# Four decoder layers with mixtures of experts: routing by 16-bit counts, one scan and one-hots in fours; first gathers inside the route; a flat norm; the mask joined with the row extreme

## The reference

```python
x = x + _L0_xattn_ref(_layernorm(x), ctx, ctx, ...)
x = x + _L0_ffn_ref(_layernorm(x), ...)     # 8 experts, 2 per row, and a shared expert
x = x + _L1_xattn_ref(_layernorm(x), ctx, ...)
x = x + _L1_ffn_ref(_layernorm(x), ...)     # 8 experts, 1 per row, bias on the router
x = x + _L2_xattn_ref(_layernorm(x), ctx, ctx, mask, ...)
x = x + _L2_ffn_ref(_layernorm(x), ...)     # two groups of 32 experts, 2 per row in each
x = x + _L3_xattn_ref(_layernorm(x), ctx, ctx, ...)
x = x + _L3_ffn_ref(_layernorm(x), ...)     # 32 experts, 1 per row, capacity 80 rows
```

```python
attn0 = jnp.where(mask, 0.0, attn).reshape(1, B * H, T, T)
attn = lax.conv_general_dilated(attn0, kernels, ..., feature_group_count=B * H, ...)
attn = jnp.where(mask, -jnp.inf, attn)
p = jax.nn.softmax(attn, axis=-1)
```

```python
expert_weights, expert_indices = lax.top_k(scores, top_k)
order = jnp.argsort(expert_indices.reshape(-1))
tok = jnp.repeat(jnp.arange(T), top_k)[order]
xs = x2[tok]
ys = lax.ragged_dot(jax.nn.silu(lax.ragged_dot(xs, wg, group_sizes))
                    * lax.ragged_dot(xs, wu, group_sizes), wd, group_sizes)
return jnp.zeros_like(x2).at[tok].add(ys * flat_w[order][:, None])
```

## Time and profile before

| | us |
|---|---|
| median of three runs | 2562.77 |
| profiled execution | 2561.07 |
| its span, first to last instruction | 2559.4 |
| TensorE matmul busy | 2060.4 (81%) |
| TensorE weight load busy | 1682.8 (66%) |
| VectorE busy | 1321.1 (52%) |
| ScalarE busy | 833.2 (33%) |
| GpSimd busy | 741.0 (29%) |

### The profile page before, as it was taken

The page is one execution under the profiler, slowest core; times in us unless marked ns, Lnnn a source line. Parts: engine busy times, 40 slices in busy tenths (PEclk is TensorE's granted clock), DMA queues, the critical chain, the costliest instruction groups (busy, mean ns, idle before and its releaser), DMA issues. The chain is left out here.

```text
span 2559.4 us, 42188 instructions
## 1 busy us (share of the span) xinstructions
PE 2060.4 (81%) x13649; PEld 1682.8 (66%) x13743; DVE 1321.1 (52%) x3816; ACT 833.2 (33%) x2012; POOL 741.0 (29%) x933
## 2 busy tenths in 40 slices
PE   6869979892799999999689847995794963787694
PEld 5657746661799988998579825664683852454594
DVE  3542225524687778887400065764546545675523
ACT  4613213412133333333323323443241432345321
POOL 1022100005344444443111032210455744231133
PEclk9869989985899999999789968996795986899797
DMA  2052130002211111100189634436377563442384
GB/s 79 9 206 63 52 113 13 1 1 86 79 34 37 42 43 38 40 22 1 40 324 347 229 109 125 129 87 231 90 154 281 159 123 100 118 125 58 136 298 167
DMA packets 142727, 280.72 MB, mean 110 GB/s; under 512 B 20160, under 2 KB 99008, under 8 KB 138432
## 3 DMA queue, kind: packets, MB, share of 16 engines
q1 hardware_dynamic: 125824, 232.49, 26.7%
q0 software_dynamic: 16704, 45.64, 7.6%
HBM read 218.94 MB, written 56.62 MB: 108 GB/s over the span
## 5 line engine op out<-in xcount | busy, mean ns | idle before, releaser
L1983 PE MATMUL heads_ps_c<-heads_band,heads_sT 128*128 128x129 f32 x3072 | 367.5, 276 | 15.1 <-DVE heads_band L2201 12.1
L1983 PEld LDWEIGHTS heads_ps_c<-heads_band,heads_sT 128*128 128x128 f32 x3072 | 362.2, 192 | 22.9 <-issue 18.9
L2139 POOL TENSOR_SCALAR heads_band<-heads_shifts,heads_taps 128x130 f32<-128x130 f32 x384 | 253.5, 675 | 268.8 <-PE heads_ps_c L1983 265.2
L1042 POOL DMA_INDIRECT experts_xg<-xn_rows,token_of x165 | 161.1, 976 | 298.9 <-PE experts_ps_x L1055 143.0
L2201 DVE SCALAR_TENSOR_TENSOR heads_band<-heads_shifts,heads_taps,heads_band 128x130 f32<-128x130 f32 x768 | 226.5, 350 | 31.7 <-POOL heads_band L2139 27.0
L2076 ACT ACTIVATE heads_probs<-heads_ps_c,heads_negmax 128x256 f32<-128x256 f32 x256 | 107.3, 470 | 371.2 <-DVE heads_negmax L2210 371.2
L1726 DVE TENSOR_REDUCE heads_negmax<-heads_ps_m 128x2 f32<-128x512 f32 x256 | 169.6, 688 | 79.7 <-PE heads_ps_m L1582 77.3
L1683 ACT ACTIVATE heads_probsT<-heads_ps_e 128x512 f32<-128x512 f32 x256 | 147.0, 596 | 193.3 <-PE heads_ps_e L1606 193.0
L1196 POOL DMA_INDIRECT combine_yg<-y_rows,slot_of x80 | 75.7, 946 | 332.7 <-SPq L66 309.3
L1066 PE MATMUL experts_ps_g<-weights_w,experts_xT 128*128 x504 | 133.6, 389 | 0.3 <-issue 0.2
L1089 PE MATMUL experts_ps_y<-weights_w,experts_hT 128*128 (+1 forms) x486 | 132.7, 382 | 1.1 <-DVE experts_y L1151 1.1
(11 more groups left out here) (389 smaller groups left out, 4442.9 us busy)
## 6 DMA issues: line engine op xcount, KB each, us to landing
experts_w<-in_experts_dram SPq DMA_DIRECT2D x23, 2180.0 KB, 10.0
weights_w<-in_experts_dram SPq DMA_DIRECT2D x16, 1536.0 KB
weights_w<-in_experts_dram SPq DMA_DIRECT2D x32, 768.0 KB, 7.4
y_rows<-experts_y SPq DMA_DIRECT2D x188, 128.0 KB, 2.2
piece_rows<-heads_pieces SPq DMA_DIRECT2D x96, 192.0 KB, 2.3
heads_stackQ<-piece_rows SPq DMA_DIRECT2D x48, 192.0 KB
heads_stackK<-piece_rows SPq DMA_DIRECT2D x48, 192.0 KB
weights_w<-in_experts_dram SPq DMA_DIRECT2D x8, 1088.0 KB
```

Source lines behind the costliest of these rows:

```text
L1042: pool.indirect_dma_start(xg[:, j % ahead, :], None, xn_dram, bass.IndirectOffsetOnAxis(ap=tb.token_of[:, j:j + 1], axis=0))\
L1983: last = pe.matmul(out[:, qc * SEQ + k0:qc * SEQ + k1], sT[:, h % 2, kc, qc * P + dq:qc * P + dq + P], band[:, h % 2, dq, w0:w0 + k1 - k0] ...
L2139: last = pool.tensor_scalar(band[:, h % 2, dq, :], shifts[:, 0, :], taps[:, r % 2, h, dq * TAPS:dq * TAPS + 1], None, ALU.mult)
```

## The change

Routes: hot becomes bf16 and lies by expert (tiles innermost); the triangle becomes `since`, 0 or -1, also bf16, so that running total plus product is the position. The count product comes first, and the zeroing of the token sum ahead of the wait. The 16 adds become one `tensor_tensor_scan` over E x 16 numbers, with a factor `restart` that is 0 at each expert's first tile. The one-hots are made four columns at a time by three instructions, double-buffered, the loop unrolled. slot_of, the capacity's mask and the tile experts come behind. POOL gathers the first three tiles of rows inside the route, as soon as token_of is there; the buffer `xg` and its semaphores belong to `FirstRows`, outside both stages.

Layer 2: the norm uses the pieces of the other norms, in groups of four tiles (`RowNorm`, L220). The weights have 40 slots; the first 8 experts of group 1 are loaded at the start of experts2_0, the other 24 in route2_1. 20 of the 32 late gathers stand in route2_1, and 12 in experts2_1 between POOL's row gathers; group 1 writes its outputs to a DRAM buffer of its own.

Convolution heads: the mask product goes. VectorE's reduction becomes two `tensor_tensor_reduce` per head, which add the mask (f32 in SBUF), write `mixes` to SBUF and take the minimum; the sign of q is turned so that the minimum is what was the negated maximum, and the exp has scale -1. TensorE's convolution waits for the row step of two heads before (`maxed`) and no longer for its exp; the row step waits for the exp of two heads before.

In the route, first TensorE's block, then VectorE's:

```diff
-            flat = hot[:, :, :].rearrange("p t e -> p (t e)")
-            pe.matmul(ps_pos.rearrange("p t e -> p (t e)"), tb.before[:, :], flat)
-            pe.matmul(ps_all.rearrange("p t e -> p (t e)"), ones[:, :], flat).then_inc(counted, 1)
-            out = ps_tok[:, 0:NT]
-            pe.sem_inc(perm_used, 4)
-            pe.matmul(out, ones[:, :], tb.zeros[:, 0:NT], start=True, stop=False, skip_group_check=True)
-            with pe.Fori(0, NK // 4) as i:
-                for p in range(4):
-                    pe.wait_ge(perm_ready, 4 * i + p + 1)
-                    pe.matmul(out, lane_hot[:, p, :], tile_hot[:, p, :], start=False, stop=False,
-                              skip_group_check=True).then_inc(perm_used, 1)
+            flat = hot[:, :, :].rearrange("p e t -> p (e t)")
+            pe.matmul(ps_all, tb.ones16[:, :], flat).then_inc(counted, 1)
+            pe.matmul(ps_pos, tb.since[:, :], flat).then_inc(placed, 1)
+            for c in range(NK // CH):
+                pe.wait_ge(chunk_ready, c + 1)
+                for n in range(CH):
+                    last = pe.matmul(out, lane_hot[:, c % 2, n, :], tile_hot[:, c % 2, n, :], start=False, stop=False,
+                                     skip_group_check=True)
+                last.then_inc(chunk_used, 1)
...
-                v.tensor_tensor(hot[:, :, :], hot_k[:, 0, :, :], hot_k[:, 1, :, :], ALU.add)\
+                v.tensor_tensor(by_tile(hot[:, :, :]), hot_k[:, 0, :, :], hot_k[:, 1, :, :], ALU.add)\
                     .then_inc(hot_ready, 1)
...
             v.wait_ge(counted, 1)
-            for t in range(TILES):
-                steps.done(v.tensor_tensor(earlier[:, t + 1, :], earlier[:, t, :], ps_all[:, t, :], ALU.add))
-            steps.done(v.tensor_tensor(pos[:, :, :], ps_pos[:, :, :], earlier[:, 0:TILES, :], ALU.add))
+            steps.done(v.tensor_tensor_scan(upto[:, :, :].rearrange("p e t -> p (e t)"),
+                                            tb.restart[:, 0:E * TILES], ps_all, 0.0, ALU.mult, ALU.add))
+            v.wait_ge(placed, 1)
+            steps.done(v.tensor_tensor(pos[:, :, :].rearrange("p e t -> p (e t)"), ps_pos,
+                                       upto[:, :, :].rearrange("p e t -> p (e t)"), ALU.add))
```

The one-hots, the tail of the route and the first rows:

```diff
+            for c in range(NK // CH):
+                if c >= 2:
+                    v.wait_ge(chunk_used, c - 1)
+                n = slice(CH * c, CH * (c + 1))
+                th, lh = tile_hot[:, c % 2, :, :], lane_hot[:, c % 2, :, :]
+                v.tensor_tensor(th, tb.row_iota[:, 0:NT].unsqueeze(1).to_broadcast([P, CH, NT]),
+                                hi[:, n].unsqueeze(2).to_broadcast([P, CH, NT]), ALU.is_equal).then_inc(own, 1)
+                steps.n += 1
+                v.tensor_tensor(lh, tb.row_iota[:, :].unsqueeze(1).to_broadcast([P, CH, P]),
+                                lo[:, n].unsqueeze(2).to_broadcast([P, CH, P]), ALU.is_equal)
+                v.wait_ge(own, steps.n)
+                v.tensor_tensor(th, th, tb.token_id[K][:, n].unsqueeze(2).to_broadcast([P, CH, NT]), ALU.mult)\
+                    .then_inc(chunk_ready, 1)
...
-            with v.Fori(0, NK // 4) as i:
-                for p in range(4):
-                    n = 4 * i + p
-                    v.wait_ge(perm_used, n + 1)
-                    v.tensor_scalar(tile_hot[:, p, :], tb.row_iota[:, 0:NT], hi[:, bass.ds(n, 1)],
-                                    tb.token_id[K][:, bass.ds(n, 1)], ALU.is_equal, ALU.mult)
-                    v.tensor_scalar(lane_hot[:, p, :], tb.row_iota[:, :], lo[:, bass.ds(n, 1)], None,
-                                    ALU.is_equal).then_inc(perm_ready, 1)
+            v.wait_ge(summed, 1)
+            v.tensor_copy(tb.token_of[:, 0:NT], ps_tok[:, 0:NT]).then_inc(token_ready, 1)
+            if capacity is None:
+                steps.done(v.tensor_tensor(ended[:, :, :], tiles_end[:, :].unsqueeze(1).to_broadcast([P, NT, E]),
+                                           tb.row_iota[:, 0:NT].unsqueeze(2).to_broadcast([P, NT, E]),
+                                           ALU.is_le))
+                steps.done(v.reduce_sum(tile_expert[:, :], ended[:, :, :], X))
+                steps.done(v.tensor_scalar(tile_expert[:, :], tile_expert[:, :], float(E - 1), float(P),
+                                           ALU.min, ALU.mult))
+                v.tensor_scalar(tb.weights_of[:, 0:NT], tile_expert[:, :], tb.column[:, 0:1], None, ALU.add)
...
+        @block.gpsimd
+        def _(pool):
+            if late is not None:
+                late.gather(pool, 0, late.EARLY, gathered)
+            if xn is not None:
+                pool.wait_ge(xn_stored, 16)
+            pool.wait_ge(token_ready, 1)
+            for j in range(first.COUNT):
+                first.gather(pool, tb, xn_dram, j)
+            if late is not None:
+                pool.wait_ge(gathered, 16 * late.EARLY)
```

The convolution heads and the late rows:

```diff
-                pe.wait_ge(exped, n + 1)
-                pe.matmul(out, ident16[:, :], mask_add[:, :], start=True, stop=False, skip_group_check=True)
+                if not (isinstance(i, int) and n < 2):
+                    pe.wait_ge(maxed, n - 1)
                 pe.wait_ge(masked, n + 3)
...
                 act.wait_ge(turned, n + 1)
                 for qc in range(QC):
-                    last = act.activation(probs[:, h % 2, qc, :], ps_c[:, h % 2, qc * SEQ:(qc + 1) * SEQ], ACT.Exp,
-                                          bias=negmax[:, h % 2, qc:qc + 1])
+                    last = act.activation(probs[:, h % 2, qc, :], mixes[:, h % 2, qc, :], ACT.Exp,
+                                          bias=least[:, h % 2, qc:qc + 1], scale=-1.0)
...
                 v.wait_ge(convolved, n + 3)
-                v.tensor_reduce(negmax[:, h % 2, :], ps_c[:, h % 2, :].rearrange("p (k n) -> p k n", k=QC), X,
-                                ALU.max, negate=True).then_inc(maxed, 1)
+                v.wait_ge(exped, n + 1)
+                v.sem_inc(rows_passed, 1)
+                for qc in range(QC):
+                    last = v.tensor_tensor_reduce(out=mixes[:, h % 2, qc, :], in0=ps_c[:, h % 2, qc * SEQ:(qc + 1) * SEQ],
+                                                  in1=mask_add[:, qc, :], scale=1.0, scalar=-NEG_BIG,
+                                                  op0=ALU.add, op1=ALU.min, accum_out=least[:, h % 2, qc:qc + 1])
+                last.then_inc(maxed, 1)
...
+            for j in range(first.COUNT, NT):
+                first.gather(pool, tb, xn_dram, j)
+                if late is not None and j % 3 == 0 and late.EARLY <= j // 3 + late.EARLY - 2 < 2 * TILES:
+                    late.gather(pool, j // 3 + late.EARLY - 2, j // 3 + late.EARLY - 1, late_in)
...
+                                   ident, ones, prefetch=lambda sp: resident.load(sp, i["experts2_1"], 0, 8, 0))
...
+            first.again(NT)
+            route_stage(core, "route2_1", logits[:, :, 32:64], 32, 2, NT, tb, ones, None, xn_dram, first, factor=0.5,
+                        prefetch=lambda sp: resident.load(sp, i["experts2_1"], 8, 32, 8), late=late)
+            resident_experts_stage(core, "experts2_1", NT, 32, [P], resident, 0, tb, first, xn_dram, y_second,
```

427 lines of the change are left out of this document (190 added, 237 removed).

## The result

The changed kernel takes 2539.24 us (median of four runs, 2534.96 to 2542.26), the kernel before 2562.63 us beside it: a ratio of 0.9899, 95% interval 0.9888 to 0.9911. That is 23 us faster, 0.9 to 1.1%. The forecast was 2505 us with a range of 2490 to 2532, so the direction was right, and the gain was 40% of what was forecast. The profiled execution is the slowest of the four runs, and has a span of 2540.5 us against 2559.4.

A forecast was written before the change was run, and what follows sets the result against it. No engine bounds the whole: TensorE paces heads1, VectorE's chain most of a route, TensorE its one-hot loop. Terms -19 - 6.6 - 1 - 8.6 - 15.8 - 5.7 - 0.5 + 0.5 = -56.7 gave 2505 us, range 2490 to 2532.

The forecast's parts named there:

- The mask in heads1: Convolution heads: one bf16 product per head goes, saving TensorE 1.28 us per round over 16 rounds; 19 us taken.
- +0.28: heads1: VectorE's extra us per head for two add-and-min with accumulator reads; bounds +0.1 (free reads) to +0.75.
- Both rivals that put VectorE at the bound: heads1: +0.75 us per head, 2516 to 2533 (chance 0.20); add-and-min at scan rate, +1.11, 2555 to 2590 (0.07).
- the one on the clock: Routes' one-hot loop: TensorE granted 2.4 GHz, total 2494 us; faster than 2495, by this or other waits going, 0.11.
- The first of those rivals: heads1: mask hidden or VectorE the bound at 4.19 us per head, saving down to about a third; chance 0.20.
- The routes up to the one-hots: route2_0 before the loop: 16-bit counts -2.47 us, scan -2.26, tile experts moved behind tokens -4.98; sum -9.9.
- I take nothing: Routes: strided write of hot and reads of pos counted at 0; bounded by doubling three 0.69 us instructions, +2 us.
- the later of the two plus some 1.2 us of barrier: Route's end: stage ends after the later of three gathers' issue and VectorE's tile experts, plus 1.2 us; route2_0 -8.6 altogether.
- The second tile: Experts behind a route: the second tile's 1.39 us wait for its rows goes; -1.2 in layer 2, -1.0 in route0, route3.
- Layer 2's experts: 12 late gathers between experts2_1's row gathers and 3 MB of prefetch in experts2_0 cost +0.5 us, 0 to +2.
- -14.6 to TensorE: route2_1: TensorE starts at 1969.4 instead of 1984.05, with 20 late gathers ahead and 24 experts loaded; -15.8 with second tile.
- Norm: Layer 2's norm: groups of four let TensorE start some 3 us sooner but add waits; -0.5, between +2 and -2.

## Why the prediction was wrong

- **The mask in heads1** (-19): right in mechanism and size. The add-and-min is the 425 ns row's, 420 ns. Its read is one instruction more and costs nothing: two of them come to 0.35 us of pitch each, 0.1 us more per head than the 0.60 of the one reduction (VectorE's busy time per head is 396.12 / 112.5 = 3.52 us, it was 3.44): the lower bound, and not +0.28. TensorE's saving, forecast at 1.28 us a round, was 1.23 in the mean. Both rivals that put VectorE at the bound fell, and so did the one on the clock: the loop took 13.73 us at 0.50 again. The first of those rivals was also priced wrong: 4.19 us per head is 33.5 a round against 34.50, which leaves three quarters of the 1.28 us and not a third, unless waits come on top. (Its 482 and 196 ns are 484 and 195 in the earlier trace rows.)
- **The routes up to the one-hots**: the counts, the scan and the tile experts behind the tokens were right. The step that failed is "I take nothing" for the strides. In route2_0 they cost 1.61 us on hot and 0.67 on picked, 2.3 us in all: above the bound of +2. Over the five routes the same two instructions are 6.6 us longer than in the trace of before, by their durations. The bound itself was wrong, as it took a doubling for the worst, and the write more than tripled. The trace bears out the rule of the Trainium skill that the prediction weighed ("Advanced Engine Details and Errata", "Memory Cachelines"), at 2.30 against 0.69 us.
- **The end of the route**: the step "the later of the two plus some 1.2 us of barrier" failed. It took a gather as done when GpSimd had issued it, but the stage's end waits until its rows have landed. The next stage starts 2.9 to 3.7 us after the last gather, and the first gather lasted 1.3 to 1.8 us longer. TensorE starts 8.46 us behind the tokens in route2_0 where 6.2 was forecast, and 9.15 in route2_1. In routes 0 and 3 it is 7.6 and 7.5 us where before had 4.5 and 4.7, which takes back over half of what VectorE's shorter chain gave. In **route1** the weights are issued 8.0 us behind the tokens, where it was 1.7: so the gain of 4.2 us turned into +1.5.
- **The second tile** (-1.2 in each): right where it was named; the wait of 1.39 us is gone. What came late next was not named: the fourth tile, by 2.37 us.
- **Layer 2's experts** (+0.5, "0 to +2"): the largest failure. It was worked out from POOL's pace and from bytes. The prefetch cost 3.9 us by standing ahead of small transfers on the same queues, and the late gathers 9.0 us, 7.8 of which went when the padding's rows were spread. Both are over the bound. Together they are 12.9 us, 12.4 more than the +0.5, of the 37.8 missing.
- **route2_1** (-14.6 to TensorE): -10.3. The tokens came 8.1 us sooner instead of 9.4, and the end of the route took the rest. That the early rows and the smaller load would free the queues in time was right: TensorE was released by the barrier, not by a transfer.
- **Norm** (-0.5): -1.6, within its bounds.
- **The range**: each term was given its own bounds, but the rivals were nearly all about heads1. No rival said that the five routes' gain is spent at their ends. One cause there, five times, is not five small independent errors. No row that the prediction used has three gathers outstanding at a barrier, and that called for a bound as wide as a transfer's own latency: in the earlier trace rows the first rows let TensorE start 2.85 us after their gather began (1816.25 to 1819.10).

## What to carry to other kernels

Work that is moved ahead of a barrier is not free because its engine is idle: a gather that is still in flight holds the barrier (here about 3 us), and in these runs it paid only where a larger transfer would otherwise stand ahead of it, and then by under 1 us. Large loads belong where nobody waits for a small transfer; count the stores behind them as well as the gathers. Look at what padding does to a memory: spread addresses that no result depends on.

## What was not expected of the hardware

- A stage's end behind outstanding indirect gathers of GpSimd: 2.9 to 3.7 us after the last one's issue ends, with three of them, 3.45 with one in route3, 0.7 us without any. GpSimd's DRAIN ends 0.08 or 0.09 us behind the landing of the last rows with one gather in the stage, 0.16 or 0.17 with three, 0.98 or 0.99 with 23 (route2_1) and 2.49 with 60 (the changed kernel's experts2_0).
- A gather's issue on GpSimd during a comparison of 128x2016 f32 with two inputs in SBUF: 2.24 and 2.71 us, against 0.95 to 0.99 without it or beside a reduction of 2.25 us with one input.
- A bf16 write of 512 elements with a stride of 32 bytes: 2.30 us against 0.69. An f32 read with a stride of 64 bytes: 0.98 against 0.64. A bf16 moving operand of TensorE, 512 columns with a stride of 64 bytes: 1.02 against 0.61.
- Gathers of 128 times the same row: DMA share 0.82 to 0.92 at 101 to 141 GB/s, against 0.46 at 135 GB/s for 128 different rows.
- The accumulator's read behind an add-and-min: 83 ns, wholly beside the next instruction; ScalarE's in the earlier trace rows is 195.
